# The sum in PSUM on 32-row strips, with the three products of each step on three different tiles

## The chip, the cores and the metric

The kernel runs on one core of one Trainium2 chip. The time is the device time of one execution in microseconds (us). Of the core's engines, TensorE (PE) multiplies matrices, VectorE (DVE), ScalarE (ACT) and GpSimd (POOL) work on elements, and SyncE (SP) issues most of the transfers.

## The reference

The input x has 16 sequences of 512 tokens with 128 channels. The block is: modulated layer norm; an attention-like layer; a gated residual; a second modulated layer norm; eight experts with the best two taken per token; another gated residual. What the change touches is the attention-like layer, here cut to its core:

```
freq  = 1 + sigmoid(wave[..., 0]) * 15            # for each token and head
phase = tanh(wave[..., 1]) * freq
offs  = phase[..., None] + freq[..., None] * (arange(32) - 16 + 0.5)
pos   = clip(token + offs, 0, 511)                # 32 taps for each token and head
gathered = interpolation of x between floor(pos) and floor(pos) + 1
bins  = clip(floor((offs + 256) / 512 * 64), 0, 63)
y     = sum over taps of kmat[bins] * gathered    # 16 channels a head
```

For a residue of tokens and a head, the kernel builds a matrix of 128 tokens x 512 positions: how many of a token's taps have passed each position, as a whole number between -16 and 16 or 0 and 32, times the tap weight of the 8-wide bin in which the position lies. That matrix is turned and multiplied with differences between neighbouring rows of x, which gives y.

## The kernel before, in words

Two sequences make a pair, and there are 8 pairs. In a pair the tokens are dealt out by their number modulo 8: residue r has 2 x 64 = 128 tokens, one on each partition. With 8 heads that makes 64 tiles for a pair and 512 tiles T in all; R numbers the 64 groups (pair, residue) of 8 heads. Every engine has its own instruction stream, written out by hand in one loop over T (r is the residue, h the head) with side work hung on given (r, h). Semaphores tie the streams together: s_p (gap product), s_n (count product), s_e (gap ready), s_dq (tap count ready), s_aw (weighted), s_at (turned), s_ev (evicted).

A tile goes through six steps:

1. PE, `gap_on` (L990): a bf16 product of 128 rows x 512 columns. The parameters of four heads lie in four strips of 32 rows; the constant `cp` has zeros in the strips of the other heads. The result lies in one of two banks of PSUM.
2. ACT, `gap` (L783): Relu with a scale for each partition, from PSUM to the SBUF ring `ee` of 4.
3. PE, `tile_on` (L995): a second such product with `cn`, into one of two other banks.
4. DVE, `counted` (L1300): product times 2^27 plus `ee`, rounded to int32, into the ring `dq` of 3.
5. DVE, `weighted` (L1310): `dq` (128x520) times the bin weights `ks`, each spread over 8 positions, into the ring `aw` of 3.
6. PE, `turn_tile` (L1003): four transposes of 128x128, into one of two banks that all transposes and `counts` take in turn (`unit`: a bank is taken when the unit two before it is evicted). ACT, `tile_evicted` (L791), copies it to `att`.

In iteration T, PE does `gap_on(T+4)`, `tile_on(T+3)`, `turn_tile(T)`, and then the side work of its head: h=0 `counts` (L981), h=1 and h=5 `weigh` (L1023, 32 matmuls on four column groups of 32), h=2 and h=4 `turn_edges` (L1010), h=3 `bins` (L954), h=7 `weigh_edges` (L1033, 16 matmuls on column groups). Once or twice a pair come `outputs` (L1045), `waves` (L947), `scores`, `ranks`, and 12 units at h=6 and h=7 that are turned or turned and copied, such as `steps_turned` (L972). ACT does `gap(T+4)`, `tile_evicted(T)`, then at h=0 `counted` (L773), at h=2 and h=4 `edge_evicted` (L798), at h=3 `copied` (L806), and at four places of a pair `centred` (L741, four activations each). DVE does `counted(T+1)`, `weighted(T)`, at h=2 `edge_terms` (L1319), at h=5 `binned` (L1290), and the statistics, the choice of experts and the residual at fixed places. SP and POOL carry the edge terms through DRAM: `edge_terms`, two stores to e_scratch, a load into `ka`, and `ends` on POOL (L621, L622), for which `turn_edges` waits.

After the loop the experts run on 135 tiles of slots, and the results are added.

Of the kernel before, what the change touches and what calls it, by code (L numbers as in the profile page):

```python
# [4 lines left out]
B, L, C = 16, 512, 128  # L5
HEADS, D, TAPS, BINS = 8, 16, 32, 64
P = 128
# [8 lines left out]
NX = 8 * NG  # L16
# [8 lines left out]
DRING = 3  # L25
AHEAD = 3
ERING = 4
SCALE = 2.0 ** 27
EXPERTS, FF = 8, 256
# [63 lines left out]
def build(nc, x, wave_wT, wave_b, kern_wT, kern_b, out_wT, w12T, w3T, gateT, cT, wmod,  # L93
# [23 lines left out]
    with ctx:  # L117
# [6 lines left out]
        def sem(name):  # L124
            return ctx.enter_context(nc.semaphore(name))

        cn = sb("cn", [P, QUAD, 512], bf16)
        cp = sb("cp", [P, QUAD, 512], bf16)
# [30 lines left out]
        dt = sb("dt", [P, 2, L])  # L159
# [16 lines left out]
        ee = sb("ee", [P, ERING, 512])  # L176
        dq = sb("dq", [P, DRING, NX], i32)
        aw = sb("aw", [P, RING, NX])
# [47 lines left out]
        stages = [stage[:, 0:QUAD * 512], stage[:, QUAD * 512:2 * QUAD * 512], stage[:, 2 * QUAD * 512:2 * QUAD * 512 + QUAD * EDGES]]  # L226
# [19 lines left out]
        ps_n, ps_p, ps_t, ps_y, side = ps[0:2], ps[2:4], ps[4:6], ps[6], ps[7]  # L246
# [20 lines left out]
        s_n, s_p, s_e = sem("count_product"), sem("gap_product"), sem("gap_ready")  # L267
        s_dq, s_aw, s_at, s_ev, s_y, s_yy = (sem("tap_count_ready"), sem("weighted"), sem("turned"), sem("evicted"),
                                             sem("y_product"), sem("y_copied"))
# [227 lines left out]
        def _(pool):  # L497
# [3 lines left out]
            pool.memset(pt[:, :, 22:ROWS], 0.0)  # L501
            pool.memset(pt[:, :, 9:12], 1.0)
            pool.memset(pt[:, :, 21:22], 1.0)
            pool.memset(dt[:, :, L - 1:L], 0.0)
# [75 lines left out]
            def params(i):  # L580
# [11 lines left out]
                pool.tensor_copy(pt[:, :, 12:21], pt[:, :, 0:9]).then_inc(s_par, 1)  # L592

            def h_steps(i):

                pool.wait_ge(s_ev, UNIT["ht", i, 1] + 1)
                if i:
                    pool.wait_ge(s_at, UNIT["dl", i - 1, 1] + 1)
                q = i % 2
                pool.tensor_tensor(rows(dt[:, 0, 0:1], [[RES, P], [1, RES - 1]]), rows(ht[:, q, 0, 0:1], [[1, P], [P, RES - 1]]),  # L600
                                   rows(ht[:, q, 1, 0:1], [[1, P], [P, RES - 1]]), ALU.subtract)
                pool.tensor_tensor(rows(dt[:, 0, RES - 1:RES], [[L, 2], [RES, HP - 1]]), rows(ht[:, q, RES - 1, 0:1], [[HP, 2], [1, HP - 1]]),
# [112 lines left out]
        def _(act):  # L715
# [59 lines left out]
            def gap(T):  # L775
# [5 lines left out]
                if T >= ERING:  # L781
                    act.wait_ge(s_dq, T - ERING + 1)
# [31 lines left out]
            for T in range(ERING):  # L814
# [744 lines left out]
```

## Time and profile before

| | |
|---|---|
| median of three runs | 1351.81 us (1351.02 to 1352.03) |
| span of the profiled execution | 1350.9 us, first to last instruction; the runs lie 0.1 to 1.1 us above it |
| loop over the 512 tiles | 41.9 to about 980 us of the span |
| PE busy, whole span | 1145.0 us, 85% |
| DVE busy | 1037.5 us, 77% |
| ACT busy | 932.5 us, 69% |
| POOL busy | 707.9 us, 52% |
| mean granted TensorE clock | 0.957 |

Busy is the union of an engine's instructions. The end of a matmul is modelled, so that PE's busy time holds the tails of matmuls too; what a matmul costs is read from the distance between starts. Shares over the whole span mix the loop with the experts' part.

### The profile page before, as it was taken

The numbers are of one execution on the slowest core, as the hardware profiler recorded it, in microseconds if no ns is written. First come the engines' busy times: TensorE is split into PE (matmuls) and PEld (weight loads), VectorE is DVE, ScalarE is ACT, GpSimd is POOL, SyncE is SP. The second block draws the span as 40 slices with busy tenths as digits, with TensorE's granted clock in tenths as the row PEclk, the third lists the DMA queues.
The fourth block names the chain that finished last, engine by engine and source line by source line (L and its number), as shares of the span: only waits on it lengthen the run. The fifth ranks groups of instructions, "written<-read, shape, count | busy, mean of one in ns | idle before, by whom it ended". The sixth has DMA issues, their size and how long they took to land.

```text
span 1350.9 us, 34980 instructions
## 1 busy us (share of the span) xinstructions
PE 1145.0 (85%) x11343; PEld 780.0 (58%) x11343; DVE 1037.5 (77%) x2316; ACT 932.5 (69%) x1906; POOL 707.9 (52%) x903
## 2 busy tenths in 40 slices
PE   4699989998998999899899989999931999999840
PEld 2366656666665666666566666666620665656520
DVE  4699999899999999999999999999942333333336
ACT  2588887888888788888888887888800555555520
POOL 5344167458457745845774584554436454555520
PEclk9899999999999999999999999999965999999975
DMA  6646455445655654554554456454512452222236
GB/s 207 164 122 178 105 148 159 125 123 174 145 133 149 159 135 121 165 153 121 159 151 141 123 147 153 131 153 118 155 61 63 115 156 72 72 72 70 68 142 253
DMA packets 213184, 181.13 MB, mean 134 GB/s; under 512 B 147600, under 2 KB 183184, under 8 KB 212112
## 3 DMA queue, kind: packets, MB, share of 16 engines
q1 hardware_dynamic: 204336, 160.99, 43.7%
q0 software_dynamic: 8672, 17.92, 3.9%
q8 instruction: 96, 1.57, 0.5%
q14 instruction: 80, 0.66, 0.2%
HBM read 96.73 MB, written 82.12 MB: 132 GB/s over the span
## 4 chain that ended last, share of the span: by engine, by line
PE 60%; DVE 11%; issue 9%; POOL 9%; ACT 5%; DMA 4%; SPq 1%; DVEq 0%; POOLq 0%; ACTq 0%
PE ps L1003 12%; PE ps L1147 8%; PE ps L1023 7%; PE ps L990 6%; PE ps L995 5%; DVE aw L1310 5%; PE ps L1162 4%; PE ps L1010 3%; PE ps L954 2%; PE ps L1033 2%; PE ps L1045 2%; PE ps L1154 2%; DMA att<-y_scratch 2%; ACT ee L783 2%; POOL slot_scratch L577 2%
## 5 line engine op out<-in xcount | busy, mean ns | idle before, releaser
L783 ACT ACTIVATE ee<-ps,f 128x512 f32<-128x512 f32 x512 | 354.3, 692 | 115.5 <-PE ps L990 111.2
L1310 DVE TENSOR_TENSOR aw<-dq,ks 128x520 f32<-128x520 int32 x512 | 416.8, 814 | 3.2 <-DMA ks<-k_scratch 3.2
L1300 DVE SCALAR_TENSOR_TENSOR dq<-ps,ee 128x512 int32<-128x512 f32 x512 | 349.9, 683 | 42.4 <-PE ps L995 39.1
L1003 PE MATMUL ps<-ident,aw 128*128 128x128 f32 x2048 | 314.6, 276 | 36.8 <-ACT att L791 19.9
L1003 PEld LDWEIGHTS ps<-ident,aw 128*128 128x128 f32 x2048 | 239.1, 141 | 180.4 <-DVE aw L1310 67.3
L791 ACT ACTIVATE att<-ps 128x512 f32<-128x512 f32 x512 | 310.0, 606 | 20.1 <-PE ps L1003 18.7
L995 PE MATMUL ps<-cn,ptt 128*128 128x512 bf16 x512 | 195.1, 381 | 10.0 <-DVE dq L1300 9.5
L608 POOL COPY kn<-kn 128x256 f32<-128x256 f32 x64 | 25.4, 396 | 337.4 <-DVE kn L1290 332.4
L711 POOL DMA_INDIRECT y_scratch<-aw,idu x135 | 129.2, 957 | 130.2 <-ACT aw L874 129.0
L990 PE MATMUL ps<-cp,ptt 128*128 128x512 bf16 x512 | 197.1, 385 | 0.0
L577 POOL DMA_INDIRECT slot_scratch<-hrow,spotu x128 | 141.4, 1105 | 44.6 <-issue 33.4
L1459 DVE TENSOR_TENSOR aw<-ee,ps 128x256 f32<-128x256 f32 x135 | 56.9, 421 | 137.3 <-ACT ee L861 137.3
L861 ACT ACTIVATE ee<-ps 128x256 f32<-128x256 f32 x135 | 51.7, 383 | 153.7 <-PE ps L1147 153.1
L1147 PE MATMUL ps<-kn,ee 128*128 x270 | 143.3, 613 | 0.4 <-DVE ee L1453 0.3
L1023 PE MATMUL ps<-att,dl 128*32 128x128 f32 x4096 | 138.4, 276 | 0.1
L1023 PEld LDWEIGHTS ps<-att,dl 128*32 128x32 f32 x4096 | 104.0, 109 | 21.6 <-ACT att L798 8.7
L1010 PE MATMUL ps<-ident,ka 128*128 128x128 f32 x512 | 78.4, 276 | 17.4 <-POOL ka L622 16.3
L615 POOL TENSOR_TENSOR kd<-kn 128x504 f32<-128x504 f32 x64 | 86.9, 1359 | 0.0
L798 ACT ACTIVATE att<-ps 128x512 f32<-128x512 f32 x128 | 77.2, 603 | 13.9 <-PE ps L1010 13.8
L1141 PE MATMUL ps<-ident,dl 128*128 128x128 f32 x135 | 38.0, 283 | 55.1 <-DMA dl<-slot_scratch 33.1
L1162 PE MATMUL ps<-hgr,aw 128*128 x540 | 82.5, 275 | 0.1
L1154 PEld LDWEIGHTS ps<-ident,aw 128*128 128x128 f32 x270 | 38.1, 142 | 71.7 <-issue 46.5
(177 smaller groups left out, 1689.7 us busy)
## 6 DMA issues: line engine op xcount, KB each, us to landing
k_scratch<-kn SPq DMA_DIRECT2D x64, 512.0 KB, 3.6
ka<-e_scratch SPq DMA_DIRECT2D x64, 512.0 KB, 3.3
ks<-k_scratch SPq DMA_DIRECT2D x128, 130.0 KB
e_scratch<-kr SPq DMA_DIRECT2D x128, 126.0 KB, 3.8
dl<-slot_scratch SPq DMA_DIRECT2D x135, 65.0 KB, 1.9
att<-y_scratch SPq DMA_DIRECT2D x16, 512.0 KB, 5.3
xc<-in_x SPq DMA_DIRECT2D x8, 512.0 KB, 6.5
h_scratch<-hx SPq DMA_DIRECT2D x16, 256.0 KB, 4.2
```

The source lines that it names most:

```text
L577: pool.indirect_dma_start(out=slots[:, :], out_offset=bass.IndirectOffsetOnAxis(ap=spotu[:, k * RES + r:k * RES + r + 1], axis=0), in_=hro ...
L711: pool.indirect_dma_start(out=yscr[:, :], out_offset=bass.IndirectOffsetOnAxis(ap=idu[:, s:s + 1], axis=0), in_=yrow[:, y, :], in_offset=N ...
L783: act.activation(ee[:, T % ERING, :], ps_p[T % 2][:, :], ACT.Relu, scale=f27[:, i % 2, r, h:h + 1]).then_inc(s_e, 1)
L791: act.activation(att[:, h, :], ps_t[UNIT["tile", T] % 2][:, :], ACT.Copy).then_inc(s_ev, 1)
L990: nc.tensor.matmul(ps_p[T % 2][:, :], params_of(T), cp[:, T % QUAD, :], start=True, stop=True).then_inc(s_p, 1)
L995: nc.tensor.matmul(ps_n[T % 2][:, :], params_of(T), cn[:, T % QUAD, :], start=True, stop=True).then_inc(s_n, 1)
L1003: last = nc.tensor.transpose(bank[:, j * P:j * P + P], aw[:, T % RING, o:o + P], ident[:, :])
L1023: last = nc.tensor.matmul(ps_y[ROWS * k:ROWS * k + ROWS, g * P:g * P + P], dl[:, R // RES % 2, j, h, :], att[:, h, j * P:j * P + P], start ...
L1147: nc.tensor.matmul(ps_h[j % 2][:, :], xT[:, j % 2, :], w12[:, bass.ds(experts[j % 8] * (2 * FF), 2 * FF)], start=True, stop=True).then_inc ...
L1162: last = nc.tensor.matmul(ps_z[j % 2][:, 0:C], hidT[:, j % 2, k * P:k * P + P], w3[:, bass.ds(experts[j % 8] * (HALVES * C) + k * C, C)], ...
L1300: nc.vector.scalar_tensor_tensor(dq[:, T % DRING, o:o + 512], ps_n[T % 2][:, :], SCALE, ee[:, T % ERING, :], ALU.mult, ALU.add).then_inc(s ...
L1310: nc.vector.tensor_tensor(aw[:, T % RING, :].rearrange("p (g k) -> p g k", k=8), dq[:, T % DRING, :].rearrange("p (g k) -> p g k", k=8), r ...
```

## The change

The three steps gap, count and sum of a tile now happen in one bank of PSUM. Four banks (`ps_s`, T modulo 4) take the place of two and two. Relu goes from the bank to the same bank; the count product then adds to it, plus a very large constant whose rounding leaves a whole number or a clipped value; a third product takes the large constant away again. DVE needs one pass, maximum and multiplication in one, which is split in two instructions where r is not 0 because the positions are now laid out by residue. `counted`, `dq` and `ee` as a ring are gone. Each product now uses only the 32 rows of its own head, and its constants are 32 rows repeated on four strips (`cn` 2x512 and `cp` 512 columns instead of 4x512 each). In iteration T the products belong to tiles T+1, T+2 and T+3, whose strips are different. PE waits for the Relu one iteration after its product; before, PE did not wait for it other than for the bank. POOL has one small instruction less in `ends`.

```diff
@@ ACT @@
-                if T >= ERING:
-                    act.wait_ge(s_dq, T - ERING + 1)
-                act.activation(ee[:, T % ERING, :], ps_p[T % 2][:, :], ACT.Relu, scale=f27[:, i % 2, r, h:h + 1]).then_inc(s_e, 1)
+                act.activation(ps_s[T % BANKS][:, :], ps_s[T % BANKS][:, :], ACT.Relu, scale=f27[:, i % 2, r, h:h + 1]).then_inc(s_e, 1)
...
-                if T + ERING < NT:
-                    gap(T + ERING)
+                if T + BANKS - 1 < NT:
+                    gap(T + BANKS - 1)
@@ PE @@
-            def params_of(T):
-                return ptt[:, T // TILES % 2, 2 * (T // HEADS % RES) + T % HEADS // QUAD, :]
+            def strip(T):
+
+                k = ROWS * (T % QUAD)
+                return slice(k, k + ROWS), ptt[k:k + ROWS, T // TILES % 2, 2 * (T // HEADS % RES) + T % HEADS // QUAD, :]
 
             def gap_on(T):
-                if T >= 2:
-                    pe.wait_ge(s_e, T - 1)
-                nc.tensor.matmul(ps_p[T % 2][:, :], params_of(T), cp[:, T % QUAD, :], start=True, stop=True).then_inc(s_p, 1)
+                if T >= BANKS:
+                    pe.wait_ge(s_aw, T - BANKS + 1)
+                at, params = strip(T)
+                nc.tensor.matmul(ps_s[T % BANKS][:, :], params, cp[at, :], start=True, stop=True).then_inc(s_p, 1)
 
             def tile_on(T):
-                if T >= 2:
-                    pe.wait_ge(s_dq, T - 1)
-                nc.tensor.matmul(ps_n[T % 2][:, :], params_of(T), cn[:, T % QUAD, :], start=True, stop=True).then_inc(s_n, 1)
+                pe.wait_ge(s_e, T + 1)
+                at, params = strip(T)
+                nc.tensor.matmul(ps_s[T % BANKS][:, :], params, cn[at, 0, :], start=False, stop=False, skip_group_check=True)
+
+            def undone_on(T):
+                at, params = strip(T)
+                nc.tensor.matmul(ps_s[T % BANKS][:, :], params, cn[at, 1, :], start=False, stop=True, skip_group_check=True).then_inc(s_n, 1)
...
-                if T + ERING < NT:
-                    gap_on(T + ERING)
-                if T + AHEAD < NT:
-                    tile_on(T + AHEAD)
+                if T + 1 < NT:
+                    undone_on(T + 1)
+                if T + 2 < NT:
+                    tile_on(T + 2)
+                if T + BANKS - 1 < NT:
+                    gap_on(T + BANKS - 1)
                 turn_tile(T)
@@ DVE @@
-                nc.vector.scalar_tensor_tensor(dq[:, T % DRING, o:o + 512], ps_n[T % 2][:, :], SCALE, ee[:, T % ERING, :], ALU.mult, ALU.add).then_inc(s_dq, 1)
...
-                dve.wait_ge(s_dq, T + 1)
+                dve.wait_ge(s_n, T + 1)
                 if T >= RING:
                     dve.wait_ge(s_at, UNIT["tile", T - RING] + 1)
-                nc.vector.tensor_tensor(aw[:, T % RING, :].rearrange("p (g k) -> p g k", k=8), dq[:, T % DRING, :].rearrange("p (g k) -> p g k", k=8),
-                                        rows(ks[:, R % 2, h, 0:1], [[1, NG], [0, 8]]), ALU.mult).then_inc(s_aw, 1)
+                src = ps_s[T % BANKS][:, :].rearrange("p (q g) -> p q g", g=HP)
+                dst = aw[:, T % RING, :].rearrange("p (q g) -> p q g", g=HP)
+                for a, b, o in ((0, r, 0), (r, RES, 1)):
+                    if a < b:
+                        ins = nc.vector.scalar_tensor_tensor(dst[:, a:b, :], src[:, a:b, :], -TAPS * SCALE,
+                                                             rows(ks[:, R % 2, h, o:o + 1], [[0, b - a], [1, HP]]), ALU.max, ALU.mult)
+                ins.then_inc(s_aw, 1)
@@ POOL, ends @@
-                pool.tensor_scalar(ka[:, R % 2, :, 0], k[:, :, LO], 16 * SCALE, None, ALU.mult)
-                pool.tensor_scalar(ka[:, R % 2, :, PADK - 1], k[:, :, LO + BINS - 1], 16 * SCALE, None, ALU.mult).then_inc(s_kf, 1)
+                pool.tensor_scalar(ka[:, R % 2, :, 0], k[:, :, LO], TAPS * SCALE, None, ALU.mult).then_inc(s_kf, 1)
```

The differences `dt` of neighbouring rows are laid out by residue too, `edge_terms` becomes one scalar_tensor_tensor of the same size, and the constants are built to match.

## Rows read from the trace of the kernel before

**Rows 1.** The page, busy shares and the span in 40 slices.

```profile
PE 1145.0 (85%) x11343; PEld 780.0 (58%) x11343; DVE 1037.5 (77%) x2316; ACT 932.5 (69%) x1906; POOL 707.9 (52%) x903
...
PEclk9899999999999999999999999999965999999975
```

**Rows 2.** Busy time of PE, PEld, DVE, ACT, POOL, clock, one pair long.

```profile
399.00:517.67 118.67, 111.44 (x1267) 77.11 (x1266) 111.61 (x227) 99.27 (x190) 73.31 (x94) 1.00 0.54 145
```

**Rows 3.** Who waited for whom in 399 to 518: us, times, longest.

```profile
PEld ps L1003 <- DVE aw L1310: 8.0, 14, 1.7
...
DVE dq L1300 <- PE ps L995: 3.9, 7, 1.0
...
PEld ps L1010 <- POOL ka L622: 2.1, 3, 1.5
```

**Rows 4.** One line that runs once a pair: first and last start, 200 to 860 us.

```profile
L1352 DVE TENSOR_TENSOR oh<-iota,topf x6: 402/402/403, 232.9 to 826.2; 128x64 f32<-128x64 f32 x6
```

**Rows 5.** The chain that ended last, 505 to 520 us: start, us, what.

```profile
509.10 0.44 PE ps L1010 x4
...
510.50 0.86 PE ps L954 x2
...
513.10 0.54 PE ps L1003 x4
513.63 1.01 PE ps L1023 x32
514.64 0.32 PE ps L990
514.97 0.22 PE ps L995
515.18 0.44 PE ps L1003 x4
...
516.49 0.60 PE ps L1033 x16
...
518.07 0.21 PE ps L981 x2
```

**Rows 6.** Instructions in order of time, 500.9 to 502.9 us: start, duration.

```profile
501.00 0.39 PE L990 MATMUL ps<-cp,ptt 128*128 128x512 bf16 x1
...
501.43 0.69 ACT L783 ACTIVATE ee<-ps,f 128x512 f32<-128x512 f32 x1 [0.59 <-PE ps L990]
501.44 0.60 PE L1003 MATMUL ps<-ident,aw 128*128 128x128 f32 x4
501.64 0.69 DVE L1300 SCALAR_TENSOR_TENSOR dq<-ps,ee 128x512 int32<-128x512 f32 x1 [0.33 <-PE ps L995]
...
502.08 0.60 ACT L791 ACTIVATE att<-ps 128x512 f32<-128x512 f32 x1
...
502.57 0.59 ACT L755 ACTIVATE dl<-ps 128x512 f32<-128x512 f32 x1
```

**Rows 7.** ACT in order of time, 418.2 to 423 us.

```profile
418.23 0.68 ACT L783 ACTIVATE ee<-ps,f 128x512 f32<-128x512 f32 x1
418.79 0.61 ACT L791 ACTIVATE att<-ps 128x512 f32<-128x512 f32 x1
...
421.05 1.82 ACT L741 ACTIVATE hx<-xc,shift,rstd 128x128 f32<-128x128 f32 x4
422.61 0.72 ACT L783 ACTIVATE ee<-ps,f 128x512 f32<-128x512 f32 x1
```

**Rows 8.** One line of DVE alone: shortest, median, longest in ns.

```profile
L1310 DVE TENSOR_TENSOR aw<-dq,ks x512: 680/690/2858, 41.2 to 978.6; 128x520 f32<-128x520 int32 x171
```

**Rows 9.** Groups of instructions by line, whole span: busy us, mean ns.

```profile
L1453 DVE COPY ee<-ps 128x128 f32<-128x128 f32 x135 | 38.2, 284 | 44.8 <-PE ps L1141 44.7
...
L1045 PE MATMUL ps<-owg,yt 128*64 128x128 f32 x512 | 32.3, 277 | 0.5 <-ACT yt L806 0.5
...
L947 PE MATMUL ps<-ww,ht 128*128 128x16 f32 x128 | 16.6, 272 | 0.7 <-ACT ht L726 0.7
```

More of the change, by code:

```diff
@@ L15 @@
 NG = L // 8 + 1
-NX = 8 * NG
 PADK = 128
@@ L24 @@
 RING = 3
-DRING = 3
-AHEAD = 3
-ERING = 4
+BANKS = 4
 SCALE = 2.0 ** 27
+GATE = 2.0 ** 90
 EXPERTS, FF = 8, 256
@@ L813, in _ @@
             counted(0)
-            for T in range(ERING):
+            for T in range(BANKS - 1):
                 gap(T)
@@ L971, in steps_turned @@
                 for j in range(NJ):
-                    last = nc.tensor.transpose(bank[:, j * P:j * P + P], dt[:, b, j * P:j * P + P], ident[:, :])
+                    last = nc.tensor.transpose(bank[:, j * P:j * P + P], dt[:, b, 2 * j:2 * j + 2, :].rearrange("p q t -> p (q t)"), ident[:, :])
                 last.then_inc(s_at, 1)
@@ L1001, in turn_tile @@
                 for j in range(NJ):
-                    o = RES - r + j * P
-                    last = nc.tensor.transpose(bank[:, j * P:j * P + P], aw[:, T % RING, o:o + P], ident[:, :])
+                    last = nc.tensor.transpose(bank[:, j * P:j * P + P], aw[:, T % RING, j * P:j * P + P], ident[:, :])
                 last.then_inc(s_at, 1)
@@ L1075, in _ @@
             counts(0)
-            for T in range(2):
+            for T in range(BANKS - 1):
                 gap_on(T)
-            for T in range(2):
-                tile_on(T)
-            gap_on(2)
-            tile_on(2)
-            gap_on(3)
+            tile_on(0)
+            undone_on(0)
+            tile_on(1)
             for b in range(2):
@@ L1360, in _ @@
             edge_terms(0)
-            counted(0)
             for T in range(NT):
@@ L1364, in _ @@
                 last, more = i - 1, i + 1 < PAIRS
-                if T + 1 < NT:
-                    counted(T + 1)
                 weighted(T)
@@ L1503 @@
     count = np.zeros((ROWS, 512))
+    undo = np.zeros((ROWS, 512))
     gap = np.zeros((ROWS, 512))
     ends = np.zeros((ROWS, EDGES))
+    reach = 1024
     for k in range(3):
-        count[3 * k:3 * k + 3] = [m, -one, -one]
+        for a, sign in ((count, 1), (undo, -1)):
+            a[3 * k:3 * k + 3] = sign * GATE / reach * np.stack([m, -one, -one])
+        count[13 + 3 * k:16 + 3 * k] = SCALE * np.stack([m, -one, -one])
         gap[3 * k:3 * k + 3] = [-m, one, one]
-        gap[12 + 3 * k:15 + 3 * k] = [m + 1, -one, -one]
+        gap[13 + 3 * k:16 + 3 * k] = [m + 1, -one, -one]
         ends[3 * k:3 * k + 3] = [edge, 0 * edge, 0 * edge - 1]
-    for a, sign in ((count, 1), (gap, -1), (ends, 1)):
+    for a, sign in ((count, 1), (undo, -1)):
+        a[9], a[10] = sign * GATE / reach * (reach - TAPS) / 2, sign * GATE / reach / 2
+        a[11], a[12] = sign * GATE * magic, -sign * GATE * magic
+    count[22], count[23], count[24], count[25] = -SCALE * eta, SCALE * magic, -SCALE * magic, -SCALE * TAPS / 2
+    for a, sign in ((gap, -1), (ends, 1)):
         a[9], a[10], a[11] = -sign * eta, magic, -magic
-    gap[21] = -0.5
+    gap[22] = -0.5
     turned = g["L0_attn_out_w"].T.reshape(HALF, QUAD, D, C)
@@ L1539 @@
         "gateT": g["L0_ffn_gate_w"].T, "cT": g["L0_c"].T, "wmod": wmod.reshape(C, 6 * C),
-        "c_n": blocks(count), "c_p": blocks(gap), "c_e": blocks(ends),
+        "c_n": np.tile(np.concatenate([count, undo], 1), (QUAD, 1)).astype(f), "c_p": np.tile(gap, (QUAD, 1)).astype(f), "c_e": blocks(ends),
         "c_tok": np.concatenate([tok[:, None] + np.arange(RES)[None, :] - 256, p[:, None]], 1).astype(f),
```

51 lines of the change are left out of this document (21 added, 30 removed).

## The prediction

> **What bounds the kernel now.** I read the page first: PE, DVE and ACT are all well used, and the granted TensorE clock is at full speed from the second slice or so to the end of the loop; it halves only where PE has almost nothing to do, in the slices just after the loop [rows 1]. So prices on PE are those of the 2.4 GHz level. Then one pair in the middle of the loop [rows 2]: DVE is busy 111.6 us of 118.67, PE 111.4 with the modelled tails of its matmuls, ACT 99.3. A line that runs once a pair comes every (826.2 - 232.9) / 5 = 118.66 us [rows 4]: the loop is periodic, 1.854 us a tile, and one pair can stand for all.
>
> Which of PE and DVE is the limit is read from the waits [rows 3]. PE waits 8.0 us a pair for `aw` from DVE; DVE waits 3.9 us for PE. With 94% busy, DVE is the tighter one, and PE waits for it mostly at the places where DVE has statistics or expert choices to do. For PE's own need I take distances between starts from the chain [rows 5]: each of the two products 0.22, a turned tile 0.44, `weigh` 1.01, `turn_edges` 0.44, `bins` 0.86, `weigh_edges` 0.60, `counts` 0.21. One thing more is to be seen there: the turned tile before `weigh` takes 0.54 and the product behind it 0.32. Going from the full array to column groups and back costs 0.10 each way.
>
> **What the change does to DVE.** Before: 0.69 for `counted` [rows 6] and 0.69 for `weighted`, whose median is 0.690 but whose longest is 2.858 us [rows 8], so that something holds it up at times. After: one pass over 512 elements, in two pieces for 7 of 8 residues. A piece costs 1.04 ns an element and 0.15 us fixed, from 284 ns for 128 elements [rows 9] and 690 for 512 [rows 6]. So 0.69 to 0.84 a tile instead of 1.38, some 0.57 x 64 = 36 us less a pair. DVE falls to about 75 of 112 us and leaves the path, but for its clumps: I keep 1.5 us a pair for the places where 2 us of expert choices stand before a `weighted`.
>
> **What it does to PE.** Two products of 0.22 become three. If strips run beside each other as the column groups do (32 matmuls in 1.01 us, far under one after another [rows 5]), the block of three lasts one product and a little for the two later starts, 0.23. But strips are another shape of the array than the transposes around them. No row shows row strips; the nearest is the column groups' 0.10 into and 0.10 out [rows 5], and I take it: every tile pays 0.10 out of the block, and 0.10 into it unless `weigh` or `weigh_edges` stood before, which paid it already. Bounds: switch 0 to 0.10, block 0.22 (all at once) to 0.66 (one after another). Steps of PE, from block to block, then are, with 0.23 + 0.10 + 0.44 + 0.10 = 0.87 for a plain one: h=0 1.08, h=1 1.88, h=2 1.31, h=3 1.73, h=4 1.31, h=5 1.88, h=6 0.87, h=7 1.47. That is 11.53 for the eight heads. The same sum before, with two products and switches only at three of eight, is 11.5 too: PE wins nothing. What it wins is the time it waited.
>
> The Trainium skill, in TensorEngine Tiling (Array Packing), Key Properties, says that changing the tiling mode drains the engine, which speaks against this change; the trace agrees for column groups, with the 0.10, and has nothing for rows. The same notes, in TensorE: Matmul & The Clock Gate, Part 3, give 3.07 times for four row strips of 512 columns. By that a block would take about 4 x 0.215 / 3.07 = 0.28 us as an estimate from that page, and the sum would come out near 1322 instead of the number below.
>
> **The new wait.** `tile_on` waits for the Relu of a product issued one iteration earlier. From the start of the product to ACT's start is 0.43, Relu takes 0.69 [rows 6], and some 0.04 pass to the next engine (0.39 of the product until 501.39, ACT at 501.43): 1.16, I take 1.17. Relu into PSUM has no row; I keep 0.69, and bound it by 0.60 (the copies of the same size) and 1.1 (both ends of one bank in each other's way, about 0.43 for a second pass). Before the Relu ACT must have done the last `tile_evicted` and its side work. Distances on ACT are 0.56 for Relu, 0.48 for an eviction [rows 6, 7], and an eviction can start 0.31 after the last of four transposes starts (501.44 + 0.33 to 502.08 [rows 6]). Going through the eight heads with these: at h=0 and h=6 the Relu decides (1.17 each), at h=2 to h=5 and h=7 PE does. At h=1 `turn_tile` finds its bank evicted 0.15 late, since ACT does Relu(3) before eviction(0). Sum: 1.17 + 2.03 + 1.31 + 1.73 + 1.31 + 1.88 + 1.17 + 1.47 = 12.07 for eight tiles, 96.6 a pair. What stands behind the waiting `tile_on` on PE is `gap_on(T+3)`, and with it ACT's next Relu, and `turn_tile`.
>
> **Side work of a pair.** `outputs` twice at 32.3 / 16 = 2.0 us [rows 9], less the slack of the steps at h=0 and h=6: 3.6. `waves` and `scores` at 16.6 / 16 = 1.0 [rows 9] and `ranks`, less slack: 2.0. Twelve units at 0.44 on PE and 0.48 on ACT: 5.3, less 1.5 of slack at h=6: 3.8. `centred` holds ACT 1.56 us, four times (421.05 to 422.61 [rows 7]); before, four Relus were done ahead and PE did not notice; now the next Relu comes late, by 0.9 after h=1 and 1.4 after h=3 in each of the two residues: 4.6. The edge terms come through DRAM in a fixed time while the period of R falls from 14.8 to some 14.0, so PE's wait of 2.1 us for `ka` [rows 3] may grow: 0.5. With DVE's 1.5: 96.6 + 3.6 + 2.0 + 3.8 + 4.6 + 0.5 + 1.5 = 112.6 us a pair against 118.67: 6.1 less.
>
> POOL's smaller `ends` and the other layout of `dt` are costed at nothing: POOL is busy 73 of 119 us [rows 2]; if that cover failed, the one `ends` instruction would give back 0.3 us for each R. Fewer bytes of constants come at the start, behind which the first norm lies: nothing. The experts' part is untouched.
>
> **The sum.** Eight pairs, of which the first begins with the transfers of its first residue: 7.9 x 6.1 = 48. From 1350.9 (span) 48 leave 1303; the median of the runs lies 0.9 above the span: 1304.
>
> **Rivals.**
> - Strips don't overlap. Then a block is 0.66 and each step that PE decides grows by 0.43, the two others by 0.24 on average, less the late eviction: 2.9 x 8 = 23 us a pair. 1304 + 7.9 x 23 = 1486. If the switch costs nothing either, 1.3 us for eight tiles come back: 1304 + 7.9 x (23 - 10.4) = 1403. This is the case on the other side; it decides from a block of about 0.23 + 6.1 / 50 = 0.35 us on, 50 being the steps of a pair in which PE decides. For it: no row has row strips. Against it: the column groups overlap.
> - Switching to strips is free. Six steps lose the 0.10 out and three the 0.10 in, of which the Relu's 1.17 takes back a little: 0.8 for eight tiles, 6.4 a pair: 1304 - 50 = 1254. Against it is the 0.10 at column groups.
> - ACT becomes the bound. It needs 99.3 us a pair by busy time [rows 2], 88% of 112.6, and the short lookahead makes each of its delays PE's. If Relu in PSUM is 0.1 slower or the delays add up as they did on DVE (94% busy and still 7 us of idle time), a pair takes 115.5 to 119.5: 1327 to 1359. At the 1.1 bound ACT alone needs 64 x 0.41 = 26 more, 125 a pair: 1400.
> - The clock. Less of the array works per matmul; PE is kept as busy in time. The trace shows the lower level only where PE stood nearly idle [rows 1]. A tenth of the loop at the lower level would cost about 90 us: 1390.
>
> **How the numbers follow.** Strips that overlap with a switch like that of column groups, 1304: 0.52. Switch free, 1254: 0.11. ACT the bound at 1327 to 1359: 0.18, a fifth of it within a hair of no change. Strips one after another, 1403 to 1486: 0.13. Relu at its upper bound or the clock, 1390 to 1400: 0.06. The range 1250 to 1362 leaves out the last two cases, 0.19. The likeliest case by itself spans 1285 to 1325, from the block's 0.28 and from 1.5 us a pair of error in the side work. Faster by over 0.2%: 0.52 + 0.11 + 0.13 = 0.76. Within 0.2%, which is about what a measurement of this kernel can tell from no change: 0.03. Slower: 0.21.
>
> **What would show it.** In the timeline the three products should start within some 20 ns of each other, once a tile, and the first transpose 0.33 us after them; a distance of 0.22 between them is the first rival, and 0.22 to the transpose the second. DVE's share in a pair should fall to about two thirds and its waits for PE grow. The waits of PE should name ACT's Relu (about 0.3 us at h=0 and h=6, and 1 us behind `centred`) where they named `aw`. A pair should take 112.6 us. What would make it wrong: a Relu that is not 0.69 us, a weight load for strips that can't be hidden, or ACT's queue running late in more steps than the two I count.

## The result and the profile after

The changed kernel takes 1335.01 us (median of 4 runs, 1333.95 to 1336.08), the kernel before 1351.41 on the same chip: ratio 0.9881, 95% interval 0.9867 to 0.9895. It is faster, but by 16 us and not by the 48 I predicted. Run again on two other chips it gave 0.9866 (0.9849 to 0.9882) and 1.0225 (1.0211 to 1.0240); what differs there comes below, under "The transfers".

The page of the changed kernel answers to [rows 1]: DVE has lost 335 us of work, PE has the same busy time as before.

```profile
span 1334.0 us, 34820 instructions
PE 1141.6 (86%) x11855; PEld 741.1 (56%) x11855; DVE 702.3 (53%) x2252; ACT 916.3 (69%) x1906; POOL 588.1 (44%) x838
...
PEclk9899999999999999999999999999955999999975
```

The line that runs once a pair [rows 4], and the windows of one pair (columns as in [rows 2]):

```profile
L1347 DVE TENSOR_TENSOR oh<-iota,topf x6: 412/414/416, 229.8 to 810.3; 128x64 f32<-128x64 f32 x6
```

```profile
387.40:503.50 116.10, 110.42 (x1334) 72.24 (x1332) 69.24 (x221) 97.50 (x190) 57.05 (x86) 1.00 0.53 149
```

A pair takes (810.3 - 229.8) / 5 = 116.1 us where it took 118.66. Inside the loop the starts of line 1000 give 115.8 for all but one of the middle pairs; one takes 117.3, with a stretch of 3.4 us at the lower clock in it. Six middle pairs give 15.5 us, the start 1.0, the experts' part 2.1; the first pair gives nothing and the last takes 1.7 longer: 16.9 of span in all. The 2.1 need not be the change's: from the last turned tile to the end, the kernels below that ran at this speed take anything from 368.8 to 371.1 us, where this one takes 369.3 and the one before 371.4.

The waits of 399 to 518 us answer to [rows 3]:

```profile
DVE aw L1303 <- PE ps L994: 44.2, 42, 2.5
...
PEld ps L990 <- ACT ps L775: 3.4, 6, 1.0
PEld ps L1000 <- DVE aw L1303: 2.8, 5, 1.0
PE ps L1000 <- ACT att L783: 2.1, 10, 0.2
```

DVE now waits for PE, PE's weight loads wait 2.8 us for `aw` where it was 8.0, and a wait for the Relu has appeared, as the prediction said. PE is still busy nearly all the time. The timeline answers to [rows 6] and shows the block:

```profile
501.54 0.39 PE L994 MATMUL ps<-cn,ptt 32*128 32x512 bf16 x1
...
501.55 0.38 PE L990 MATMUL ps<-cn,ptt 32*128 32x512 bf16 x1
501.55 0.39 PE L985 MATMUL ps<-cp,ptt 32*128 32x512 bf16 x1
...
501.87 0.66 PE L1000 MATMUL ps<-ident,aw 128*128 128x128 f32 x4
```

Three products start within 10 ns, and the first transpose 0.32 to 0.33 us behind them: 0.22 of the product and 0.10 of the switch.

To say where the time is, I cut the loop into residues of eight heads, from the first transpose of a tile h=0 to the next one (starts of line 1000, 1003 before). In us, a middle pair:

| | r0 | r1 | r2 | r3 | r4 | r5 | r6 | r7 | sum |
|---|---|---|---|---|---|---|---|---|---|
| before | 15.24 | 14.38 | 16.06 | 15.20 | 16.79 | 13.32 | 15.12 | 12.56 | 118.7 |
| after | 14.29 | 14.71 | 15.44 | 14.84 | 15.37 | 13.32 | 15.10 | 12.74 | 115.8 |

The gain, 3.4 us, lies in r0, r2, r3 and r4, residues in which DVE has statistics and expert choices to do; r1 and r7 lose 0.5. The residues in which PE has nothing beside the tiles and the side work of every residue are r1 and r5 of the last pair; I call them plain: 12.85 and 12.83 us before, 12.61 in both after. r7 of the other pairs went the other way, from 12.56 to 12.74, and r5 stayed at 13.32. So work without clumps of DVE has won next to nothing.

### The profile page after: what moved, and what is told of

It reads as the page before. It is cut to its first block and busy times, and to the rows that moved or that the text cites. A ratio compares the mean times of both kernels' runs of the same rounds, so it can differ in the third digit from the quotient of the medians.

```text
span 1334.0 us, 34820 instructions
## 1 busy us (share of the span) xinstructions
PE 1141.6 (86%) x11855; PEld 741.1 (56%) x11855; DVE 702.3 (53%) x2252; ACT 916.3 (69%) x1906; POOL 588.1 (44%) x838
## 5 line engine op out<-in xcount | busy, mean ns | idle before, releaser
L1303 DVE SCALAR_TENSOR_TENSOR aw<-ps,ks 128x64 f32<-128x64 f32 (+7 forms) x960 | 382.0, 437 | 387.4 <-PE ps L994 342.8
L775 ACT ACTIVATE ps<-ps,f 128x512 f32<-128x512 f32 x512 | 343.4, 671 | 131.2 <-PE ps L985 131.2
L1000 PE MATMUL ps<-ident,aw 128*128 128x128 f32 x2048 | 332.9, 285 | 31.6 <-ACT att L783 15.9
L783 ACT ACTIVATE att<-ps 128x512 f32<-128x512 f32 x512 | 310.2, 606 | 11.5 <-PE ps L1000 11.2
L1000 PEld LDWEIGHTS ps<-ident,aw 128*128 128x128 f32 x2048 | 216.3, 141 | 157.9 <-issue 134.4
L990 PE MATMUL ps<-cn,ptt 32*128 32x512 bf16 x512 | 198.8, 388 | 13.9 <-ACT ps L775 13.9
L994 PE MATMUL ps<-cn,ptt 32*128 32x512 bf16 x512 | 198.7, 388 | 0.0
L985 PE MATMUL ps<-cp,ptt 32*128 32x512 bf16 x512 | 197.9, 389 | 0.0
L573 POOL DMA_INDIRECT slot_scratch<-hrow,spotu x128 | 127.3, 995 | 48.2 <-issue 33.4
L994 PEld LDWEIGHTS ps<-cn,ptt 32*128 32x128 bf16 x512 | 46.4, 91 | 124.6 <-issue 121.2
L1151 PEld LDWEIGHTS ps<-ident,aw 128*128 128x128 f32 x270 | 38.0, 141 | 71.6 <-issue 46.4
```

Source lines behind the costliest of these rows:

```text
L573: pool.indirect_dma_start(out=slots[:, :], out_offset=bass.IndirectOffsetOnAxis(ap=spotu[:, k * RES + r:k * RES + r + 1], axis=0), in_=hro ...
L775: act.activation(ps_s[T % BANKS][:, :], ps_s[T % BANKS][:, :], ACT.Relu, scale=f27[:, i % 2, r, h:h + 1]).then_inc(s_e, 1)
L783: act.activation(att[:, h, :], ps_t[UNIT["tile", T] % 2][:, :], ACT.Copy).then_inc(s_ev, 1)
L985: nc.tensor.matmul(ps_s[T % BANKS][:, :], params, cp[at, :], start=True, stop=True).then_inc(s_p, 1)
L990: nc.tensor.matmul(ps_s[T % BANKS][:, :], params, cn[at, 0, :], start=False, stop=False, skip_group_check=True)
L994: nc.tensor.matmul(ps_s[T % BANKS][:, :], params, cn[at, 1, :], start=False, stop=True, skip_group_check=True).then_inc(s_n, 1)
```

## The experiments

**Strips against the full array.** Three kernels, on one chip (before there: 1374.01 us; the changed kernel did not run beside them). x1_full has zeros around each tile's 32 rows of constants and multiplies with all 128 rows; x2_full_two leaves the third product out of it; x3_strip_two leaves it out of the changed kernel. The last two leave the sum unrounded and the wrongly counted taps in it.

```
-  k = ROWS * (T % QUAD); matmul(ps_s, ptt[k:k+ROWS, ...], cn[k:k+ROWS, 0, :])
+  matmul(ps_s, ptt[:, ...], cn[:, T % QUAD, 0, :])          # x1, x2
-  undone_on(T + 1)                                          # x2, x3, with the large constant GATE at 0
```

> The changed kernel with its three products on all 128 rows (constants of zero in the other heads' strips), so one after another and with no change of the array's shape; all else as changed. Theory A, that a block of strips costs what it saves in switches (0.22 for the three, 0.10 in, 0.10 out and some 0.05 in the first transposes, against 0.645 for three full products in a row): a step that PE decides grows by about 0.17 to 0.27, the two Relu steps to 1.37, eight tiles from 12.6 to about 13.9, 10 us a pair: 1417 us. Rival B, that switching is nearly free and the new waits for ACT ate the gain: each step that PE decides grows by the whole 0.43, 20 us a pair: 1495 us.

> As the run with full products, but with the third product left out and the large constant taken from the second (the sum is left unrounded, so the output is another one): the two full products of before, with the order and the waits of the changed kernel. Theory A: two full products (0.43) cost PE what three strips with their switches do, so 1335 to 1340 us. Rival B: slower than the strips by 0.21 in each step that PE decides, 1415 us.

> The changed kernel with the third product left out and the large constant taken from the second (output another one), strips as changed. Both theories: the third product runs beside the others, so 1335 us within 3. If strips share something and only two fit beside each other, faster by up to 40 us.

Measured: x1_full 1468.40 us (1.0679, 1.0661 to 1.0697), x2_full_two 1437.67 (1.0467, 1.0449 to 1.0485), x3_strip_two 1434.04 (1.0420, 1.0395 to 1.0444). The timeline of x1_full shows each product waiting for the one ahead:

```profile
499.87 0.38 PE L1002 MATMUL ps<-cn,ptt 128*128 128x512 bf16 x1
500.08 0.38 PE L998 MATMUL ps<-cn,ptt 128*128 128x512 bf16 x1
500.30 0.38 PE L993 MATMUL ps<-cp,ptt 128*128 128x512 bf16 x1
500.51 0.60 PE L1008 MATMUL ps<-ident,aw 128*128 128x128 f32 x4
```

Block to turn is 0.64 there, with no cost of a switch, against 0.32 on strips. Plain residues (last pair, r1): 14.15 with three full products, 13.29 with two, 12.58 with two on strips, 12.61 with three. The third product costs 0.03 us in eight tiles on strips, 0.87 on the full array. So three strips take the time of one, as assumed, and their gain over full products is larger than their switches. The totals of this chip are higher for another reason, below, and can't be read against the times expected; 14.15 lies near the 13.9 of theory A. For x2 I had expected 12.6, and 13.29 is a miss: with full products the gap product starts 0.23 us behind the count product, the Relu with it, and in r1 of the last pair PE's weight loads wait 1.2 us for the Relu, where they wait 0.2 with strips. The new order of the steps costs something by itself, and strips win part of that back.

**What relief for DVE is worth.** x4_before_light is the kernel before with `counted` on 64 of its 512 columns, so that the rest of the counts is not added up.

> The kernel before with DVE's first pass (count product times scale plus gap) on 64 of the 512 columns only, the rest of its output left stale: 0.47 us less of DVE in each tile, 30 us a pair, all else unchanged. Theory A (before, DVE's load cost PE only some waits, and PE's own need is 106 us a pair): a pair takes 108 to 110 us instead of 118.7, 1275 us. Rival B': before was bound by PE and ACT in most steps already, so that relief of DVE alone is worth no more than the change brought: 1335 us.

Measured: 1363.96, ratio 0.9905 (0.9874 to 0.9936), on the same chip as x1 to x3, whose totals are raised. What the chip left undisturbed is r0 to r6 of the second pair, 14.43, 14.37, 15.40, 14.82, 14.87, 13.32, 15.21, and r7 of the first, 12.56. The gain lies in r0, r2, r3 and r4, 3.7 us a pair; from the third pair on r2 is 16.13 and r4 14.99, which leaves 2.9. These are the residues in which the change won, and 2.9 is what it won in all. So the change gains about what relief of DVE gives with PE's work left as it was (rival B' of this run), and theory A's 108 to 110 us a pair fails.

In the middle pairs r5 and r7 do not move (13.32, 12.56), though DVE is busy 94% of the time [rows 2] and PE waits for `aw`. In the last pair r5 does: 12.83 before, 12.37 with the relief, 12.61 with the change. There DVE did hold a plain residue, by 0.46 us, of which the change won only 0.22: from the turn of h=6 to the next it takes 1.27 us before, 0.87 in x4, and 1.18 in the changed kernel, where the Relu decides.

**Centring on DVE, and a shorter eviction.** Four kernels on one chip (before there: 1372.89). y2_centred_dve does both calls of `centred` by DVE's `tensor_scalar`. y3 and y4 evict only 64 of 512 columns of each turned tile from the second pair on, in the changed kernel and in the one before; the rest of `att` keeps its old contents.

```
-  act.activation(att[:, h, :], ps_t[...][:, :], ACT.Copy)
+  act.activation(att[:, h, 0:64], ps_t[...][:, 0:64], ACT.Copy)   # y3, y4, from the second pair on
```

> The changed kernel itself once more, beside the three others of this call: 0.988 of the kernel before, if the chip behaves as in the first comparison. Every other run of this call is read against it.

> The changed kernel with `centred`, four times four activations a pair, moved from ACT to DVE at the same heads (a tensor_scalar each); DVE stands idle over 40 us of a pair. Theory A (PE now waits for ACT's Relu wherever ACT has a long piece of side work): residues 1 and 2 fall from 14.7 and 15.4 us by some 2 us each, 3.5 to 4 us a pair, 28 to 31 us in all. Rival (these residues are bound by PE's own work): no change.

> The changed kernel with ACT's eviction of a tile on 64 of 512 columns from the second pair on (the rest of `att` is left stale), which shortens the way from a turned tile to the free bank by 0.37 us and relieves ACT by as much. Theory C: in a plain residue (12.6 us) it isn't the switches nor DVE but this round trip that is added to PE's 11.5 us: turn_tile(T+1) waits for the eviction of tile T wherever a unit stands between, so the residue falls to about 12.1, and residues 1 and 2 by 2 us more: 5 to 6 us a pair, 35 to 45 us in all. Theory A alone (PE's own work with its switches): the plain residue stays at 12.6, and only 15 us are won at `centred`.

> The kernel before with the same shortened eviction (64 of 512 columns from the second pair on, the rest stale). Theory C: the plain residues of before (12.56 and 13.3 us) were held by the same round trip, not by DVE, and fall to 11.8 and 12.6; residues with DVE's clumps don't: 3 to 4 us a pair, 25 to 30 us. Theory A (before was held by DVE and its waits): no change over 5 us.

Measured: y1_after 1404.32 (1.0225, 1.0211 to 1.0240), y2 1406.23 (1.0236, 1.0214 to 1.0259), y3 1369.29 (0.9974, 0.9955 to 0.9993), y4 1366.33 (0.9956, 0.9941 to 0.9971). Two findings.

First, residues r2 to r5 of y1_after in the middle pairs are those of the first chip to 0.01 us, but for one with the lower clock there, while r6, r7, r0 and r1 are up to 4.3 us longer. Second, in y3 the undisturbed r5 falls from 13.32 to 12.68, the turns up to h=6 start 0.32 us after their block (h=1 took 0.57, h=3 and h=5 0.43), and r2 falls to 13.7. y4 wins 0.5 in r5 and r7 as well, but nothing in r5 of the last pair, where DVE decides. Elsewhere the eviction is on the path of both kernels. r5 of the last pair falls by 0.26 in y3, from 12.61 to 12.35, half of what I expected. y2 won 1.8 us in r1 (2.1 in the first pair) and lost 2.1 in r2.

**The transfers.** On the chip where the changed kernel lost, engines stand still together. The timeline of y1_after, one place:

```profile
516.20 1.02 POOL L573 DMA_INDIRECT slot_scratch<-hrow,spotu  x1 [0.17 <-issue]
...
516.94 0.66 PE L1000 MATMUL ps<-ident,aw 128*128 128x128 f32 x4
517.53 0.97 POOL L573 DMA_INDIRECT slot_scratch<-hrow,spotu  x1 [0.30 <-issue]
519.32 0.60 ACT L749 ACTIVATE dl<-ps 128x512 f32<-128x512 f32 x1 [3.06 <-remote]
519.36 0.76 DVE L1303 SCALAR_TENSOR_TENSOR aw<-ps,ks 128x448 f32<-128x448 f32 x2 [3.70 <-remote]
...
520.06 0.38 PE L973 MATMUL ps<-ce,ptt 128*128 128x252 bf16 x2 [2.47 <-ACT dl L749]
```

PE's products ended at 517.0 and its transposes at 517.6, but DVE and ACT begin at 519.3: the increments of the semaphores are recorded that late. I compared the end of each instruction with the next record of its semaphore. More than 0.3 us lie between them for 13 of 6316 instructions of the changed kernel on the first chip and for 788 of 6316 in y1_after. Some of the 788 are not late but missing: in y1_after 627 increments have no record of their own, and the next one is taken. The standstill itself is seen in the timeline. In the loop of y1_after 228 lie 1 to 6 us apart, and 121 of these have at least eight increments of the indirect transfers in between (16 belong to each transfer); of stretches of the same lengths put down at random, 11% do. z2_burst and z4_before_burst issue the indirect transfers in r5 to r7 (two residues' worth, three, three).

```
-  r5+5: 0 | r6: 1, +5: 2 | r7: 3, +5: 4 | next r0: 5, +6: 6 | r1: 7
+  r5+5: 0 1 | r6: 2, +5: 3 4 | r7: 5, +5: 6 7
```

z3_burst_centred adds y2's centring.

> The changed kernel itself once more, as the yardstick for the kernels beside it, since its time differs from chip to chip (1335 and 1404 us) while its residues r2 to r5 do not. If increments of semaphores are again recorded late on this chip, r6, r7, r0 and r1 of the pairs from the second on are 0.5 to 4 us longer than 13.1 to 15.1 us and the time lies near 1404; if this chip is like the first one, it lies near 1335 and the pairs last 115.8 us.

> The changed kernel, but the sixteen indirect transfers of a pair are issued in r5, r6 and r7 (two residues' worth, then three, then three) where they were spread over r5 to the next r1. Theory, the late increments come with these transfers: r0 and r1 fall to 14.3 and 14.7 us in every pair, r6 and r7 grow in turn, and the time moves by less than 15 us in either direction. Rival, the late increments belong to something else that happens around the change of pairs (the loads of the next pair's rows): r0 and r1 stay 1 to 4 us above that. On a chip without late increments both expect 1335 to 1340 us.

> As z2_burst, and the two centring operations of ACT (r1, r2) moved to DVE as in y2_centred_dve. There r1 fell to 12.6 us and r2 rose to 17.5, where DVE stood behind the wait for the indirect transfers of the pair before. Theory: with these done by the end of r7, DVE doesn't wait, r1 is 12.6 us, r2 falls below 15, and the time is 7 x 2 to 7 x 4 = 14 to 28 us below z2_burst. Rival: r2 was long for another reason (the second norm's work on POOL or the semaphores of the sums), then r2 stays near 17.5 and the time is that of z2_burst.

> The kernel before with the same move of its indirect transfers. Theory of the transfers: as in z2_burst the time lost to late increments moves out of r0 and r1 into r6 and r7, with a total within 10 us of the kernel before on this chip. Rival: nothing moves. On a chip without late increments both expect a time within 3 us of the kernel before.

Measured, on a chip without late increments (before: 1352.61): z1_after 1334.64 (0.9866), z2 1335.35 (0.9875, 0.9856 to 0.9893), z3 1331.17 (0.9844, 0.9825 to 0.9863), z4 1351.75 (0.9995, 0.9985 to 1.0005). So these runs could not tell the two theories of the transfers apart, but they settled another thing. In z3, r1 is 12.9 and r2 17.5, although the transfers are done by r7: the wait for them is not what made r2 long, and my theory of y2 falls. One line of DVE in r2, and the timeline of that place with POOL's work:

```profile
L1251 DVE TENSOR_SCALAR hrow<-xo,rstd,shift x8: 328/334/1429, 535.0 to 542.2; 128x128 f32<-128x128 f32 x8
```

```profile
534.89 1.27 POOL L527 TENSOR_TENSOR hx<-hx,mb 128x512 f32<-128x512 f32 x1
534.96 4.09 DVE L1251 TENSOR_SCALAR hrow<-xo,rstd,shift 128x128 f32<-128x128 f32 x4 [0.26 <-POOL shift L521]
...
536.23 1.27 POOL L528 TENSOR_TENSOR hx<-hx,mb 128x512 f32<-128x512 f32 x1
...
537.67 1.29 POOL L527 TENSOR_TENSOR hx<-hx,mb 128x512 f32<-128x512 f32 x1
...
539.76 0.53 PEld L969 LDWEIGHTS ps<-ident,aw 128*128 128x128 f32 x4 [2.79 <-DVE aw L1288]
```

Four operations of 0.33 take 4.09 us: three of them take 1.28 to 1.43 and end within 0.09 us of one of POOL's, and PE waits 2.8 us behind. The half at h=3, when POOL was through, took 0.33 each. The Trainium skill, in SBUF — State Buffer, SBUF: two separate sides, says that a DVE operation in a two-port mode, or with two inputs in SBUF beside a GpSimd operation that reads SBUF, shares a pair of ports with GpSimd, and that whichever starts first holds the pair for its whole instruction. The shared ends in the trace agree; which of the two conditions this operation meets, no row tells.

**Moving work with that in mind.** On a fourth chip (before: 1351.68). a1_centred_one moves only r1's centring to DVE; a2_centred_later also r2's, at h=3 and h=5, meant to lie behind POOL's products. a3_evict_two gives the evictions of odd heads to DVE, with a semaphore of their own; a4_both is a2 with a3.

```
 weighted(T)
+if more and (r, h) in ((1, 1), (1, 3)): centred(0, i + 1, h // 2)   # a1, a2, a4
+if i and (r, h) in ((2, 3), (2, 5)): centred(1, last, h // 4)       # a2, a4
+if the eviction of T - 1 is here: tile_evicted(T - 1)               # a3, a4
```

> The changed kernel with only the centring of the next pair's rows (r1, at h=1 and h=3) moved from ACT to DVE; the one of r2 stays on ACT. From z3_burst_centred: r1 falls from 14.71 to 12.9 us and r2 stays at 15.44, 1.8 us a pair in seven pairs: 12 to 13 us less than the changed kernel, 1322 on a chip where that takes 1335. If r2 was not long because of its own centring on DVE but because r1 had been short (work put off, not won), r2 rises to 17.5 here too and the time stays within 3 us of the changed kernel.

> As a1_centred_one, and the centring of r2 on DVE as well, but at h=3 and h=5, behind POOL's four tensor_tensor of 1.27 us each. In z3_burst_centred the first of these operations of DVE took 1.28 and 1.43 us instead of 0.33, and ended each with one of POOL's. Theory, the two engines shut each other out of SBUF there: now they take 0.33 each, r2 falls to 13.4 to 14.5 us, and the time is 6 to 14 us below a1_centred_one. Rival, r2 waits for the norm's inputs or for POOL in turn, which comes later now: r2 stays at 15.4 to 17.5, and the time is that of a1_centred_one or more.

> The changed kernel, but the turned tiles of odd heads are evicted by DVE (except in three places where DVE has expert choices to do), right behind the weighting of the next tile; ACT keeps the others. Theory, the order of Relus and evictions on ACT and the round trip through two banks hold the residues: the late turns at h=1, h=3 and h=5 vanish (0.5 us a residue), the Relus come on time, and the plain residue falls from 12.61 to 11.8 to 12.2 us, the pair from 115.8 by 4 to 8: 1273 to 1305 us where the changed kernel takes 1335. Rival, PE's own steps hold it: plain residue 12.5 to 12.6 and 1330 to 1340 us. A third: DVE's evictions come late behind its side work, and the time is above 1340.

> a2_centred_later and a3_evict_two together. If they hold in different residues or heads they add up: the sum of both gains within 8 us, 1260 to 1300 us. If DVE gets too full in r1 and r2 (r1: five evictions and statistics, centring 2.3 us), the gain of a2 is lost again and the time is that of a3_evict_two.

Measured: a1 1321.16 (0.9775, 0.9759 to 0.9791), a2 1316.74 (0.9745, 0.9729 to 0.9761), a3 1322.50 (0.9785, 0.9769 to 0.9802), a4 1330.18 (0.9836, 0.9820 to 0.9853). a1 has r1 12.91 and r2 15.43, as expected; a2 has r2 14.96, half of a microsecond better and not the one to two that I expected. The trace of a2 shows why: in the pair below two of the eight operations of r2 still run beside POOL's products and take 1.40 and 1.42 us instead of 0.34, each ending within 0.09 us of one of POOL's. The line over the whole loop (shortest, median, longest in ns):

```profile
L1262 DVE TENSOR_SCALAR hrow<-xo,rstd,shift x56: 330/337/1423, 189.8 to 874.7; 128x128 f32<-128x128 f32 x56
```

12 of the 56 take 1.37 us or more. A place later still was not tried. a2 is all the same the fastest kernel of this study, 2.5% under the kernel before. The windows of one of its pairs:

```profile
385.50:499.05 113.55, 109.01 (x1333) 71.70 (x1330) 75.31 (x234) 91.62 (x173) 57.37 (x85) 1.00 0.56 151
```

a3 won 1 us each in r1 and r2, where ACT had been short of time, and lost 0.5 in r4; its plain residue stayed at 12.61, with all its steps unchanged to 0.01. But a3 moved the wrong evictions to judge the theory by: the turns of h=1, 3 and 5 wait for those of h=0, 2 and 4. In a4 DVE is busy 92.3 of 115 us, r1 and r2 go up to 14.1 and 15.4, and the gains don't add up: the time is above that of either.

**The right evictions.** b1_evict_even gives those of h=0, 2 and 4 to DVE; b2_centred_burst is a2 with the transfers of z2. The chip was one with late increments (before: 1378.14).

> The changed kernel with the evictions of h=0, 2 and 4 on DVE, behind the weighting of the next tile. Theory A, ACT's queue order makes them late: turns at h=1, h=3 and h=5 start 0.32 us after their block (now 0.60, 0.43, 0.43) and the plain residue falls by 0.5 to 12.1 us. Theory B, the round trip: the weighting starts about 0.38 after the block and takes 0.69 to 0.76, the transposes end about 0.85 after it, so the eviction starts at 1.1 on DVE as it does on ACT, takes 0.68 instead of 0.60, and the plain residue is 12.6 to 12.9 us. The time then gains only what ACT's relief gives in r1 and r2, 1315 to 1330 where the changed kernel takes 1335.

> a2_centred_later with the indirect transfers of a pair issued in r5 to r7 as in z2_burst. On a chip without late increments: within 4 us of a2_centred_later (1317), ratio 0.972 to 0.977, which confirms the best version. On a chip with late increments: if they come with the transfers, r0 is 14.3 us and r1 12.9 in every pair (y2_centred_dve: 15.9 to 18.4 and 14.5 to 16.1), and r6 and r7 are longer by 1 to 6 us; if they belong to something else at that place, r0 and r1 stay long.

Measured: b1 1428.80 (1.0368, 1.0347 to 1.0389), b2 1421.61 (1.0298, 1.0275 to 1.0321). In b1's undisturbed r5 the steps at h=2 and h=4 from turn to turn are 1.60 us (changed kernel: 1.46; y3: 1.35), and r5 is 13.62 (changed kernel: 13.32); the plain residue, r5 of the last pair, is 13.03, slightly over the 12.6 to 12.9 of theory B and far from the 12.1 of theory A. So theory B holds: an eviction costs a round trip, whichever engine does it. The time of b1, on this chip, says nothing of the 1315 to 1330 expected. In b2, r1 is 12.91 us in every pair, as on a chip without late increments, while r6 takes 21.1, r7 19.2 and r0 18.0 (means of the third to sixth pair; y1_after: 17.8, 16.4, 16.9, and r1 16.4). The delay has left r1 with the transfers; r0 still has what those of the end of r7 bring. It sits in the first two heads of each of these residues, 2.5 to 5.5 us in the first, right behind the transfers' issue.

## Why the prediction was right and wrong

**Right.** The side, and the mechanism in its parts: the three products start together, the switch costs 0.10 each way, Relu into PSUM takes 0.67 (0.69 taken), DVE left the path in the middle pairs but for its clumps, and waits of PE name ACT. Rival "strips one after another" is x1_full, and "switch free" is ruled out by the 0.32 before each turn. That 1335 lies in the range of 1250 to 1362 is luck more than foresight: it lies outside the 1285 to 1325 of the case that I described, and inside those of another, ACT as the bound, which holds only in part.

**The step that failed** is the term of 12.07 us for eight plain tiles, 96.6 a pair, and behind it the sentence "PE wins nothing. What it wins is the time it waited": I let PE's waits for `aw` stand for time to be won in every residue. A plain residue of the changed kernel takes 12.61. Its steps from block to block (three products and what follows them), in us:

| | h=0 | h=1 | h=2 | h=3 | h=4 | h=5 | h=6 | h=7 | sum |
|---|---|---|---|---|---|---|---|---|---|
| predicted | 1.17 | 2.03 | 1.31 | 1.73 | 1.31 | 1.88 | 1.17 | 1.47 | 12.07 |
| r1 of the last pair | 1.13 | 2.23 | 1.35 | 1.86 | 1.35 | 2.01 | 0.91 | 1.78 | 12.61 |

At h=6 and h=7 the wait for the Relu falls into the next step, 2.69 for both against 2.64. Of the 0.54 us that I had too few:
- Some 0.37 are turns that wait for their bank. They start 0.66, 0.43 and 0.43 us behind the block at h=1, 3 and 5 where the others take 0.32, so late by 0.34, 0.11 and 0.11; I had 0.15 for the first and nothing for the others. y3, with the short eviction, has none of this.
- Some 0.17 are in PE's own steps. Behind a switch the fourth transpose starts 0.384 us after the first and not 0.327, a cost of the switch of 0.06 that I had not seen in [rows 5].

The sum that I set beside it for the kernel before was wrong as well. The prices of [rows 5] give eight times 0.88 for a tile's products and turn, 4.57 for the side work of the eight heads and 0.60 for the switches, 12.2 us and not 11.5; x4, with DVE relieved, shows 12.37. By my own prices eight plain residues would have won some 8 x 0.14 = 1.1 us, and 5 of the 6.1 us a pair had to be waits; x4 shows that 2.9 to 3.7 were there.

The timeline of a plain residue shows the late turn:

```profile
871.15 0.66 PE L1000 MATMUL ps<-ident,aw 128*128 128x128 f32 x4
...
871.30 0.66 ACT L775 ACTIVATE ps<-ps,f 128x512 f32<-128x512 f32 x1 [0.34 <-PE ps L985]
871.65 0.38 PE L973 MATMUL ps<-ce,ptt 128*128 128x252 bf16 x2
871.88 0.59 ACT L783 ACTIVATE att<-ps 128x512 f32<-128x512 f32 x1
871.96 0.38 PE L994 MATMUL ps<-cn,ptt 32*128 32x512 bf16 x1
...
872.62 0.63 PE L1000 MATMUL ps<-ident,aw 128*128 128x128 f32 x4 [0.21 <-ACT att L783]
```

Between two turns with another unit between them both banks are in use, and the second turn waits for the eviction of the first: 0.73 from the turn to the eviction, 0.59 for it, 0.15 to PE, 1.47 us. Before, with the same round trip, it was 1.38: a turn at 501.44, its eviction from 502.08 to 502.68 [rows 6], the next turn at 502.82. PE's own work for that step, 1.35 (y3), fits into it with little slack. A shorter block of products could win nothing there, and the later eviction costs 0.1.

In a pair: 8 x 0.54 = 4.3 us less gain than predicted. The side work came to 115.8 - 8 x 12.61 = 14.9 instead of 16.0, 1.1 more gain. 112.6 + 4.3 - 1.1 = 115.8.

**Terms of the side work.** `centred` was right in kind: blocks wait 0.61 to 0.66 us behind its first half and 1.04 to 1.09 behind its second, 3.4 in the two residues where I had 4.6. With the late turns that follow, r1 and r2 are 2.1 and 2.0 longer than without it (first pair of y2, last pair of a2). a2 gets 2.3 a pair of it back, 1.8 of them as a1 does. Waves and scores take twice the 1.0 that I had for each: the 16.6 us [rows 9] are for eight calls, and I divided by 16. The expert choices still hold PE up 0.8 at r4.

**DVE's load** fell by 335 us, where 36 a pair made 288. The rest has an explanation that [rows 8] held: 109 of the 512 `weighted` of before were over 1.3 times the median, 57 us too much in all. They read both tensors from SBUF. All 109 ran beside a tensor_tensor of POOL, and none of the 304 without one beside it was long; 99 ran beside one and were not. The new `weighted` reads one of its two tensors from PSUM, and its longest is 693 ns. POOL has lost 120 us of busy time as well (707.9 to 588.1). One of its lines, before and after, same shape (busy us, mean ns of one):

```profile
L615 POOL TENSOR_TENSOR kd<-kn 128x504 f32<-128x504 f32 x64 | 86.9, 1359 | 0.0
...
L611 POOL TENSOR_TENSOR kd<-kn 128x504 f32<-128x504 f32 x64 | 65.6, 1026 | 0.0
```

I had costed POOL's side at nothing, for another reason, its idle time; what this relief is worth was not tried by itself.

**The factor 7.9** was too high: the first pair won nothing and the last lost 1.7. There a stretch at the lower clock takes 1.5 (r4 of the last pair 16.05, in z2_burst 14.53) and the last seven steps take 1.65 more than before, against 1.4 won in the rest; I read the 1.65 as the longer chain of a tile, which stands bare when no later products are left, but no run tries it. 6 pairs x 2.6 and 1.4 from the ends make the 16.9.

**The clock**, the last rival, holds to a small part. The profile of the changed kernel has two stretches of 3.4 us at the lower level in the loop, where that of the kernel before has none, and each costs 1.5 us (r4 of one middle pair 16.88, of the others 15.36).

**ACT the bound** was the rival that came nearest in its number (1327 to 1359), but a3 shows ACT relieved of 15 us a pair and the plain residue unmoved. It is a bound in r1 and r2, where a3 wins 1.0 each. The late turns of plain residues wait for ACT's eviction, but b1 shows that giving it to another engine makes them later.

## What to carry to other kernels

A wait with a large total is worth what the residues or stages in which it stands last are worth: cut the loop into its stages, find the plainest one, and ask which engine or round trip sets that before summing waits over a period. An engine that is busy 94% of the time can be the limit in one stage and not in the next. Work that has been taken off one engine is worth as much again when it makes room for the work of another: moving `centred` won 18 us, as much as the change by itself. Which place it is moved to counts: beside POOL's products an operation of DVE on SBUF took 1.3 to 1.4 us instead of 0.33.

## What the runs showed of the hardware

- In three of the six sets of runs, each on one chip, semaphore increments were recorded up to some 3 us late near the landings of indirect transfers. The kernel before takes 1351 to 1353 us in the other three sets and 1373 to 1378 in these; the changed kernel took 1335 in two of the first kind and 1404 in one of the second. In the three sets with late increments 568 to 705 of the 6320 to 6832 increments of the engines have no record of their own, in the others 13 to 28; of the 2176 increments by which the indirect transfers to `slot_scratch` tell of their landing, 877 to 1240 are recorded, in the others 2091 to 2165. I read the difference in time so: with a lookahead of one tile the changed kernel has no slack for such a delay, where the kernel before had four Relus ahead; that reason was not tested by itself. Why the chips differ, whether the transfers cause the delay or something that goes with them, and whether the number of increments or of bytes does it, stays open.
- The clock dropped to its lower level for 3.4 us at a time in the loop: twice in the profile of the changed kernel (from 570 us, where PE had been busy, and from 915 us), once in that of z2_burst, never in that of the kernel before, and in z3 after each stall in r2. The windows of z3 at that place, with the granted clock in the last column but two:

```profile
534.00:538.00 4.00, 3.06 (x48) 1.90 (x47) 3.75 (x6) 3.37 (x6) 3.67 (x8) 1.00 0.83 237
538.00:542.00 4.00, 2.24 (x11) 1.49 (x11) 4.00 (x9) 1.02 (x3) 2.23 (x2) 0.75 0.07 13
542.00:546.00 4.00, 3.96 (x24) 2.42 (x22) 2.64 (x9) 3.10 (x7) 0.03 (x1) 0.82 0.34 65
```

- Products on 32-row strips of three tiles start 3 to 10 ns apart where none of them waits; the array's switch costs 0.10 us on either side and 0.06 between the first two transposes behind it. The Trainium skill, in TensorEngine Tiling (Array Packing), Key Properties, says that changing the tiling mode drains TensorE; the trace agrees and gives its price here.
